# A hyperbolic transformer block on one core: VectorE's loop cut at another place, diagonals made by ScalarE, and a symmetric product by its upper blocks

## The reference

```python
ada = t_emb @ w_ada + b_ada          # six modulation vectors per sequence
xm  = expmap0(layer_norm(logmap0(x)) * (1 + sc_msa) + sh_msa)
q, k, v = heads of plin(xm, w, b)    # plin(x, w, b) = expmap0(logmap0(x) @ w + b)
attn_out = plin(softmax(q k^T / 4) v, w_o, b_o)      # 16 heads of 16
x1  = mobius_add(x, expmap0(g_msa * logmap0(attn_out)))
xm  = expmap0(layer_norm(logmap0(x1)) * (1 + sc_mlp) + sh_mlp)
ff  = plin(plin(xm, w_f1, b_f1), w_f2, b_f2)         # 256 to 1024 to 256, no activation between
return x + mobius_add(x1, expmap0(g_mlp * logmap0(ff)))
```

## Time and profile before

| what | us |
|---|---|
| median of 3 executions | 864.21 |
| lowest, highest | 862.32, 869.98 |
| the profiled execution | 866.16 |
| its span in the trace | 864.40 |
| TensorE busy | 729.1 (84%) |
| VectorE busy | 682.3 (79%) |
| ScalarE busy | 557.0 (64%) |
| GpSimd busy | 405.4 (47%) |

### The profile page before, as it was taken

The page is one execution under the profiler, slowest core; times in us unless marked ns, Lnnn a source line. Parts: engine busy times, 40 slices in busy tenths (PEclk is TensorE's granted clock), DMA queues, the critical chain, the costliest instruction groups (busy, mean ns, idle before and its releaser), DMA issues.

```text
span 864.4 us, 30460 instructions
## 1 busy us (share of the span) xinstructions
PE 729.1 (84%) x9429; PEld 525.6 (61%) x9429; DVE 682.3 (79%) x2219; ACT 557.0 (64%) x1513; POOL 405.4 (47%) x810
## 2 busy tenths in 40 slices
PE   5967988898888988888989888805889999979987
PEld 2746777677776777777767677602345555545556
DVE  3787888788887888878888887476899998878971
ACT  1126777777777777777777777535667776756751
POOL 1005555555555555555555555211245645635644
PEclk9979999999999999999999999657889999999999
DMA  9921111111111111111111110023425444535412
GB/s 325 350 67 51 57 55 45 50 50 55 55 50 48 48 55 55 55 48 45 53 55 55 54 42 19 17 61 82 125 86 146 135 124 134 147 100 146 134 62 86
DMA packets 51818, 74.04 MB, mean 86 GB/s; under 512 B 7081, under 2 KB 34609, under 8 KB 51762
## 3 DMA queue, kind: packets, MB, share of 16 engines
q1 hardware_dynamic: 49970, 70.55, 27.4%
q10 hardware_dynamic: 1792, 2.89, 0.9%
HBM read 64.24 MB, written 9.18 MB: 85 GB/s over the span
## 4 chain that ended last, share of the span: by engine, by line
PE 38%; DVE 23%; issue 19%; POOL 6%; DMA 4%; SPq 3%; DVEq 2%; ACT 2%; POOLq 0%; ACTq 0%
PE p_qkv L872 20%; PE p_oz L846 8%; DVE u L1134 7%; PE p_s L862 3%; SPq L348 3%; DVE g_all L1169 2%; DMA x_all<-in_x 2%; PE p_oz L840 2%; DMA mod<-mod_rows 2%; DVEq L50 1%; PE p_s L937 1%; DVE qk L1209 1%; DVE junk L1176 1%; DMA mod_b<-mod_rows 1%; POOL rt L483 1%
## 5 line engine op out<-in xcount | busy, mean ns | idle before, releaser
L872 PE MATMUL p_qkv<-wqkv,tT 128*128 128x256 f32 x768 | 194.7, 390 | 33.8 <-DVE u L1134 33.5
L872 PEld LDWEIGHTS p_qkv<-wqkv,tT 128*128 128x128 f32 x768 | 135.1, 192 | 64.9 <-DVE u L1134 25.3
L457 POOL TENSOR_TENSOR qk<-qk 128x512 f16<-128x512 f32 x64 | 73.9, 1155 | 146.0 <-ACT qk L604 146.0
L886 PEld LDWEIGHTS p_o<-v,pT 64*64 64x64 f32 x4096 | 68.9, 137 | 36.1 <-issue 36.1
L1162 DVE TENSOR_TENSOR z<-p_oz,bo 128x256 f32<-128x256 f32 x64 | 27.2, 425 | 78.8 <-PE p_oz L846 78.6
L609 ACT ACTIVATE qkT<-p_s 128x1024 f32<-128x1024 f32 x64 | 65.5, 1023 | 33.4 <-PE p_s L829 33.4
L886 PE MATMUL p_o<-v,pT 64*64 64x17 f32 x4096 | 73.4, 210 | 12.0 <-ACT pT L654 12.0
L654 ACT ACTIVATE pT<-p_s 128x1024 f32<-128x1024 f32 x64 | 65.5, 1023 | 20.6 <-PE p_s L862 20.6
L1134 DVE SCALAR_TENSOR_TENSOR u<-p_qkv,ct,bqkv 128x768 f32<-128x768 f32 x64 | 65.1, 1018 | 14.9 <-issue 12.9
L846 PE MATMUL p_oz<-wo,oT 128*128 128x256 f32 x256 | 75.2, 418 | 0.6 <-ACT oT L614 0.5
L829 PE MATMUL p_s<-ident,qk 128*128 128x128 f16 x1024 | 68.7, 221 | 6.5 <-issue 4.3
(11 more groups left out here) (263 smaller groups left out, 1774.3 us busy)
## 6 DMA issues: line engine op xcount, KB each, us to landing
mod<-mod_rows SPq DMA_DIRECT2D x128, 128.0 KB, 2.8
x_all<-in_x SPq DMA_DIRECT2D x8, 1024.0 KB, 14.3
gate<-mod_rows SPq DMA_DIRECT2D x128, 64.0 KB, 2.5
mod<-mod_rows SPq DMA_DIRECT2D x32, 256.0 KB, 4.0
mod_b<-mod_rows SPq DMA_DIRECT2D x32, 256.0 KB, 4.0
out<-x_all SPq DMA_DIRECT2D x32, 256.0 KB, 2.2
gate<-gate_rows SPq DMA_DIRECT2D x32, 128.0 KB, 2.9
bqkv<-gate_rows SPq DMA_DIRECT2D x32, 128.0 KB, 3.3
```

Source lines behind the costliest of these rows:

```text
L457: pool.tensor_tensor(low, qk[:, :].rearrange("p (a h d) -> p a h d", a=2, d=HD), qk4[:, :, :, 0, :], ALU.subtract).then_inc(low_ready, 1)
L872: mm = pe.matmul(p_qkv[:, a * D:a * D + D], tT[:, k, c, :], wqkv[:, c, a * D:a * D + D], start=c == 0, stop=c == C - 1)
L886: mm = pe.matmul(p_o[S * e:S * e + S, col:col + VW], pT[keys, e, g, :], v[keys, k, 2 * g + e, :], start=True, stop=True, skip_group_check= ...
```

## The change

It has three parts.

1. VectorE's attention loop is cut elsewhere. The slot is split in `slot_until_rows` (project to sum_rows) and `slot_from_bias` (add_bo to dot_x). `run_slots_rotated` runs the same operations in the same order, but a turn of the loop (27 of them) begins at add_bo and ends with sum_rows of the next slot. `split_ff_bias` is called at the end of slot 67 instead of at the start of slot 2.
2. The diagonals are made by ScalarE (Copy of ident with a scale by partition) instead of GpSimd (tensor_tensor). They stand behind evac_t2T and ahead of evac_out.
3. The norm's block of wff holds the upper blocks of G alone: for c = 0 the first diagonal block and twice the upper right one, for c = 1 the second diagonal block. The columns of wff are ordered norm, output, norm (128, 256, 128), so that the matmul for c = 1 takes 384 columns instead of 512. The setup's products, the bias row, inner_square and mlp_output follow this order, and ScalarE makes 8 copies instead of 7.

```diff
+        OUT_COLS = slice(P, P + D)
+        NORM_COLS = slice(0, 4, 3)
...
+        def run_slots_rotated(eng, first_part, second_part, first, items, slots):
+
+            for s in range(first):
+                first_part(s // 2, s % 2)
+                second_part(s // 2, s % 2)
+            first_part(first // 2, 0)
+            with eng.Fori(first // 2, items // 2 - 1) as h:
+                second_part(h, 0)
+                first_part(h, 1)
+                second_part(h, 1)
+                first_part(h + 1, 0)
+            second_part(items // 2 - 1, 0)
+            for s in range(items - 1, slots):
+                first_part(s // 2, s % 2)
+                second_part(s // 2, s % 2)
...
-            def diagonals(i, k, q, col, g):
-
-                pool.wait_ge(al2_ready, g + 1)
-                pool.wait_ge(be2_ready, g + 1)
-                after(pool, out_psum, i - 1)
-                for j in range(2):
-                    for n, fac2 in enumerate((al2, be2)):
-                        pool.tensor_tensor(diags[k][j][n], ident[:, :], fac2[:, q, col + j:col + j + 1].broadcast_to([P, P]),
-                                           ALU.mult).then_inc(diag_ready, 1)
...
             for m in range(C):
-                act.activation(wff[:, m, 0:D], p_s[:, m * 512:m * 512 + D], ACT.Copy).then_inc(ffw_made, 1)
-                act.activation(wff[:, m, D:2 * D], s_bank[2 + m][:, 0:D], ACT.Copy).then_inc(ffw_made, 1)
...
+                act.activation(wff[:, m, OUT_COLS], p_s[:, m * 512:m * 512 + D], ACT.Copy).then_inc(ffw_made, 1)
+                act.activation(wff[:, m, 3 * P * m:3 * P * m + P], s_bank[2 + m][:, m * P:m * P + P], ACT.Copy).then_inc(ffw_made, 1)
+            act.activation(wff[:, 0, 3 * P:4 * P], s_bank[2][:, P:2 * P], ACT.Copy, scale=2.0).then_inc(ffw_made, 1)
...
+            def diagonals(i, k, q, col, g):
+
+                act.wait_ge(al2_ready, g + 1)
+                act.wait_ge(be2_ready, g + 1)
+                after(act, out_psum, i - 1)
+                for j in range(2):
+                    for n, fac2 in enumerate((al2, be2)):
+                        act.activation(diags[k][j][n], ident[:, :], ACT.Copy, scale=fac2[:, q, col + j:col + j + 1]).then_inc(diag_ready, 1)
...
                 if on2(h, off, M_Q):
                     evac_t2T(slots - M_Q, (off - M_Q) % 2)
+                if on2(h, off, M_D):
+                    diagonals(slots - M_D, (off - M_D) % 2, parity(off, M_D), 2 * ((off - M_D) % GROUP),
+                              (TURN // GROUP) * h + (off - M_D) // GROUP)
                 if on2(h, off, M_O):
                     evac_out(slots - M_O, (off - M_O) % 2)
...
-                inner_sum(s_bank[2 + m][:, 0:D], w1Tm, lambda fc: w1T[:, fc, :])
+                inner_sum(s_bank[2 + m][:, m * P:D], w1Tm, lambda fc: w1T[:, fc, m * P:D])
...
-                    mm = pe.matmul((p_qkv, p_s)[k][:, 512 * j:512 * j + 512], t2T[:, k, j, c, :], wff[:, c, :], start=False, stop=c == C - 1)
+                    mm = pe.matmul((p_qkv, p_s)[k][:, 512 * j + c * P:512 * j + 512], t2T[:, k, j, c, :], wff[:, c, c * P:2 * D],
+                                   start=False, stop=c == C - 1)
...
-            def slot(h, off):
-                if isinstance(h, int) and 2 * h + off == 2:
-                    split_ff_bias()
+            def slot_until_rows(h, off):
...
+            def slot_from_bias(h, off):
...
+                if isinstance(h, int) and 2 * h + off == T + 3:
+                    split_ff_bias()
+
+            run_slots_rotated(dve, slot_until_rows, slot_from_bias, FIRST, T, T + L_L)
...
-                dve.scalar_tensor_tensor(out=junk2[:, 3, j, :], in0=(p_qkv, p_s)[k][:, 512 * j + D:512 * j + 2 * D], scalar=1.0,
-                                         in1=t2s[:, k, j, :], op0=ALU.mult, op1=ALU.mult,
+                dve.scalar_tensor_tensor(out=junk2[:, 3, j, :].rearrange("p (b n) -> p b n", n=P), in0=(p_qkv, p_s)[k][:, 512 * j:512 * j + 512].rearrange("p (b n) -> p b n", n=P)[:, NORM_COLS, :],
+                                         scalar=1.0, in1=t2s[:, k, j, :].rearrange("p (b n) -> p b n", n=P), op0=ALU.mult, op1=ALU.mult,
```

More of the change, by code:

```diff
@@ L517, in slot2 @@
                     output_roots(group_at(h, off, M_N), parity(off, M_N))
-                if on2(h, off, M_D):
-                    diagonals(slots - M_D, (off - M_D) % 2, parity(off, M_D), 2 * ((off - M_D) % GROUP),
-                              (TURN // GROUP) * h + (off - M_D) // GROUP)
                 if on2(h, off, M_A):
@@ L891, in slot @@
                 if isinstance(h, int) and 2 * h + off == 2:
[L892 removed]
+                    pe.wait_ge(ffw_made, 8)
                 if on(h, off, L_H):
```

11 lines of the change are left out of this document (5 added, 6 removed).

## The result

The changed kernel takes 859.54 us in the median (856.25 to 863.43, 20 runs), the kernel before 862.97 us on the same chips: a ratio of 0.995 (95%: 0.9932 to 0.9968). I forecast 852.8 us, 11.4 us less; 3.4 came. The direction was right, the size was not.

A forecast was written before the change was run, and what follows sets the result against it. TensorE and VectorE bound attention as a ring; TensorE and the chain through store and load bound the MLP. Gains of 11.7, 1.8 and 1.5 less losses of 1.65 and 2.0 made 11.4 us: 852.8 us, range 843 to 863.

The forecast's parts named there:

- The rotated loop, 11.7 us: Attention loop: moving VectorE's branch ahead of add_bo saves 0.43 us in each of 27 turns, 11.7 us.
- There 0.99 us of idleness covers its 0.48 us, and 0.5 stay: Ahead of add_bo, VectorE's 0.99 us wait for TensorE was to hide the loop branch's 0.48 us.
- the ring: Attention chain: project_o, VectorE's add_bo through dots to project, TensorE's next qkv to project_o; branch adds 0.48 us per two slots.
- the pair is 14.92 us, the forecast: Two attention slots of about 7.46 us each, instead of 15.36 us for both.
- The moved split, +1.65 us: End of attention: split_ff_bias at slot 67 delays the scores by 1.65 us; its removal from slot 2 gains nothing.
- The symmetric block and the MLP sum: MLP: 384 columns give back 0.43 us a slot; with diagonals, six groups of four lose 2.0 us.
- The group is 31.26 us against 7.47+23.46 = 30.93: MLP loop: a group of four slots becomes 0.33 us longer, 2.0 us over six groups.
- The first slots: MLP ahead of slot 8: three slots with TensorE slow gain 0.6 us each, 1.8 us in all.
- the end: MLP's end: a shorter last inner product and seven small operations without diagonals beside them gain 1.5 us.
- Diagonals on ScalarE: MLP slots: four diagonals at 0.29 us cost ScalarE 1.17 us a slot; VectorE's stretch beside GpSimd goes, 0.56 us a slot.
- this chain and its lag: MLP: transposes, evac_t2T, evac_out, SyncE's store, load, scale_t2; lag grows from 7.64 to 8.81 us.

The follow-up runs named there:

- e1: Kernel before with VectorE's rotated attention loop alone, split_ff_bias still at slot 2: 858.25 us, 0.9939 of the kernel before.
- e7: Changed kernel with split_ff_bias back at slot 2: 853.23 us, 0.9856 of the kernel before.
- e2: Changed kernel with add_bo's three waits reordered, z_psum last in both halves of the turn: 856.16 us, 0.9908 of the kernel before.
- e12: Changed kernel with ScalarE's diagonals behind evac_out in the loop, ahead of it in the last nine slots: 848.92 us, 0.9829 of the kernel before.
- e6: Changed kernel with SyncE issuing the store of out one slot later: 850.38 us, 0.9823 of the kernel before.
- e19: Changed kernel with split at slot 2, later store, waits ordered by halves, MLP loop written out, diagonals back on GpSimd: 833.29 us, 0.9657 of the kernel before.
- e18: Changed kernel with split at slot 2, store one slot later, waits ordered by halves, MLP loop written out: 827.27 us, 0.9582 of the kernel before.
- e3: Kernel before with the diagonals moved from GpSimd to ScalarE, ahead of evac_out, alone: 864.87 us, 1.0005 of the kernel before.

## Why the prediction was right or wrong, point by point

**The rotated loop, 11.7 us.** The branch went where I said, and its 0.48 us ahead of `project` are gone. The step that failed is "There 0.99 us of idleness covers its 0.48 us, and 0.5 stay", taken as the whole cost of a turn's bookkeeping. A turn also works out semaphore counts from its register, and two of them stand between z_psum's wait and z. They put 0.16 us on the ring (0.20 from project_o's end to z, and not 0.04), and a part of the gap of 0.08 us ahead of the other `project` (200.16) goes the same way. So a pair fell by 0.24 us and not by 0.43, and 6.7 us came for 11.7. With the order changed by halves the pair is 14.92 us, the forecast: the idleness does cover the branch, once the counts are worked out in it too.

**The moved split, +1.65 us.** The step that failed is "a loss of 1.65 us". The longer slot came in about that size (8.83 us for 7.42), but I priced only VectorE's delay and not what the wait does to TensorE's clock: 3.31 us for o, where e1 without the split waits 0.30. Moving it back gave 6.3 us: 1.4 for the slot and 5 for slots at half the clock, which the kernel before, by its mean clock, ran whole in most executions. The profile that I worked from had its clock at 0.51 in just this stretch, so the trace seemed to show the end of attention as it always is. It was one of the minority, some 3 us over the median; the difference I put down to scatter.

**The symmetric block and the MLP sum.** The block's records shrank as forecast, eight in 3.27 us for 3.70, and so did TensorE's slot, 7.04 us for 7.47. "The group is 31.26 us against 7.47+23.46 = 30.93" was near: the ordinary groups of e7 and e2 (without the turn's and the one behind it) last 29.8 to 31.8 us, and 24 slots take 191.3 to 191.6, not 193.4. The first slots gave 0.8 and not 1.8 us, the end 1.9 and not 1.5. In all -2.6 us where the terms make -1.3. The +5.9 us in the profile after is no part of it: the same MLP code took 191.27 and 191.56 us in e7 and e2, whose turn groups last 35.4 and 35.3 us and not 38.3. An episode of the clock is what I'd have explained, had I taken that profile alone. It may not be rare: of the 20 executions of the changed kernel 8 have a mean clock of 0.950 or less, the profiled one among them, and take 860.1 to 863.4 us; the other 12 take 856.3 to 859.7. No other profile of this kernel shows what sets the 8 apart.

**Diagonals on ScalarE.** 0.29 us from start to start, 1.17 a slot, and 0.48 us for scale_t2 in place of 0.61: both as forecast. So was the chain that they lengthen, by evac_out, store and load; e12 and e6 cut it in two places and gave 10.6 and 9.2 us. I had named this chain and its lag (8.81 us forecast, mostly 8.2 to 9.5 measured), and not seen that the kernel before lost 5.1 us to it.

The sum by the runs: -6.7 for the rotation, +5.6 for the last nine slots in most executions (58.7 to 64.3), -2.6 for the MLP: -3.7 us, for 3.4 less measured and 11.4 forecast. Of the 7.7 us between the two sums the rotation makes 5.0 and the end of attention 4.0, and the MLP gives 1.3 back. That -3.7 meets 3.4 so closely is in part luck: the same MLP code took 191.35 us in the profile before and 194.55 in e1's for the 24 slots. The level was off as well: I counted from a median of 864.21 us (3 executions), and 20 executions gave 862.97, so the forecast is 6.7 us off where the gain is 8.0 short.

In e19 and e18, which differ only in who makes the diagonals, VectorE's operation of the rows above takes 582 ns beside GpSimd's and 479 without. The Trainium skill's rule ("SBUF — State Buffer", "Who interferes with whom") is that a VectorE instruction with two SBUF inputs contends with a GpSimd instruction that reads SBUF, and the trace agrees.

At the loop's turn the trace shows an issue gap of 4.4 us that goes when the loop is written out. The Trainium skill has that a taken branch whose target lies outside the window of instructions that the engine holds stalls until they are fetched ("Runtime: NRT & Kernel Launch", "Instruction fetch mechanics"). The trace agrees in that the gap goes with the branch; no row of it shows a fetch.

## What to carry to other kernels

Ahead of the wait that ends last, put every other wait of the instruction, above all those whose count comes from a loop's register; then measure each place, since one of two here was better the other way. Work that is moved into a stretch where TensorE already waits isn't priced by its length alone: compare the granted clock of several executions before taking one profile as the stretch's cost. And where two transfers share an issuing queue, ask whether the later one needs anything that the earlier one waits for.

## What the runs showed that I had not expected

- TensorE's clock at the end of attention came in two ways from one program: 17 of 29 executions of the kernel before had a mean of 0.96 or more, and in profiles of the same attention code (e3's and the one before) that is 58.6 against 63.7 us for the same nine slots.
- Two turns of a loop with eight slots cost 10.2 us more than the same slots written out. The slot of the one branch back shows about 5 (12.88 against 7.73 us), and the slot behind it, with TensorE's clock down, 1.6 (8.68 against 7.05). Another 1.6 are the first seven MLP slots (48.21 against 46.62), which e18, written out as well, doesn't have (48.25). The rest lies mostly in the late slots of the other groups (8.64 against 7.73). I haven't shown what it is; counts from registers, as in attention, are a guess.
